# Two 64-row tiles for the values and scores of a cross-attention layer, and the sum of the values' halves in HBM

## What is computed

```python
q = x @ Wq + bq                       # 32 query heads of 32
k = ctx @ Wk + bk; v = ctx @ Wv + bv  # 8 key/value heads of 32, each shared by 4 query heads
p = softmax(q k^T / sqrt(32) + mask)  # over 64 keys
x = layernorm((p v) @ Wo + bo + x) * gamma + beta
```

## Time and profile before

| | |
|---|---|
| median of 3 runs | 1740.94 us |
| profiled execution, device time | 1740.28 us |
| its span in the profile | 1738.5 us |
| TensorE (PE) busy, share of the span | 98% |
| weight loads (PEld) | 82% |
| VectorE (DVE) | 67% |
| GpSimd (POOL) | 61% |
| ScalarE (ACT) | 33% |
| granted TensorE clock, mean | 0.998 |
| chain that ended last | PE 86%, DVE 6%, POOL 3%, DMA 2%, ACT 1%, issue 2% |

### The profile page before, as it was taken

One profiled execution on the slowest core, in us unless ns is written; L12 is line 12 of the kernel. 1 busy time (PEld: TensorE's weight loads), 2 busy tenths in 40 slices (PEclk: granted clock), 3 DMA queues, 4 the chain that ended last, 5 costly groups with the idle time before them and its releaser, 6 DMA issues.

```text
span 1738.5 us, 22384 instructions
## 1 busy us (share of the span) xinstructions
PE 1709.0 (98%) x8449; PEld 1428.8 (82%) x8449; DVE 1169.7 (67%) x1111; ACT 581.3 (33%) x669; POOL 1060.6 (61%) x587
## 2 busy tenths in 40 slices
PE   6999999999999899999999999999999999999998
PEld 6888888888888788888888877888888888888887
DVE  7999898898988656565656578446644664466443
ACT  4444354444444433333434223122312231223110
POOL 1777877877787766565766553446734673467331
PEclk9999999999999999999999999999999999999999
DMA  8443344332336577777776856556545654565432
GB/s 240 103 110 86 77 110 108 80 86 73 77 98 187 165 228 230 222 232 227 240 224 223 262 176 194 172 167 185 172 152 169 184 171 154 170 184 168 132 109 97
DMA packets 278127, 280.11 MB, mean 161 GB/s; under 512 B 62330, under 2 KB 230404, under 8 KB 278020
## 3 DMA queue, kind: packets, MB, share of 16 engines
q1 hardware_dynamic: 276672, 276.97, 52.6%
q10 hardware_dynamic: 1348, 1.71, 0.3%
HBM read 175.81 MB, written 102.76 MB: 160 GB/s over the span
## 4 chain that ended last, share of the span: by engine, by line
PE 86%; DVE 6%; POOL 3%; issue 2%; DMA 2%; ACT 1%; SPq 0%; POOLq 0%; DVEq 0%; ACTq 0%
PE ps L53 28%; PE ps L54 27%; PE ps L55 27%; PE ps L712 1%; PE ps L720 1%; POOL y L1428 1%; POOL xb L1414 1%; DMA ocr<-o_scratch 1%; POOL wqsl L1446 0%; DVE xT0r L1039 0%; DVE wq0l L1058 0%; DMA pd<-p_scratch 0%; DMA p_scratch<-prob 0%; DMA ctx<-in_ctx_dram 0%; PE ps L693 0%
## 5 line engine op out<-in xcount | busy, mean ns | idle before, releaser
L1465 POOL TENSOR_TENSOR x2Tl<-x2r,x2Th 128x1024 fp32r<-128x1024 f32 x31 | 74.5, 2404 | 275.1 <-ACT x2Th L972 275.1
L1244 DVE STREAM_TRANSPOSE x2r<-xd 128x1024 f32<-128x1024 f32 x32 | 68.8, 2150 | 200.6 <-PE ps L55 200.6
L1399 POOL TENSOR_TENSOR pr<-pr,small 128x1024 f32<-128x1024 f32 x64 | 121.9, 1904 | 97.3 <-DVE small L1132 97.2
L972 ACT CAST x2Th<-x2r 128x1024 fp32r<-128x1024 f32 x32 | 33.7, 1052 | 366.5 <-DVE x2r L1244 366.5
L1394 POOL TENSOR_TENSOR pr<-pr,small 128x1024 f32<-128x1024 f32 x64 | 121.9, 1905 | 11.3 <-DVE small L1110 9.2
L1414 POOL TENSOR_TENSOR xb<-xb,bo 128x1024 f32<-128x1024 f32 x32 | 76.9, 2402 | 71.7 <-DMA xb<-in_x_dram 71.6
L1428 POOL TENSOR_TENSOR y<-y,bet 128x1024 f32<-128x1024 f32 x31 | 74.4, 2400 | 56.9 <-DVE y L1162 56.9
L1106 DVE TENSOR_REDUCE small<-pr 128x16 f32<-128x1024 f32 x64 | 78.1, 1220 | 42.6 <-ACT pr L852 42.6
L53 PE MATMUL ps<-wo0h,oc0l 128*128 128x512 f32 x256 | 102.0, 398 | 0.0
L53 PE MATMUL ps<-wo0h,oc1l 128*128 128x512 f32 x256 | 101.6, 397 | 0.4 <-DVE y L1199 0.4
L53 PE MATMUL ps<-xT0h,wq0l 128*128 128x512 f32 x256 | 100.1, 391 | 1.1 <-DVE wq0l L1058 1.1
(11 more groups left out here) (381 smaller groups left out, 5441.9 us busy)
## 6 DMA issues: line engine op xcount, KB each, us to landing
xr<-in_x_dram SPq DMA_DIRECT2D x128, 128.0 KB, 2.9
o_scratch<-ot SPq DMA_DIRECT2D x256, 64.0 KB, 1.8
ocr<-o_scratch SPq DMA_DIRECT2D x16, 1024.0 KB, 7.7
xb<-in_x_dram SPq DMA_DIRECT2D x32, 512.0 KB, 6.6
a_scratch<-ost SPq DMA_DIRECT2D x64, 256.0 KB, 3.5
b_scratch<-ost SPq DMA_DIRECT2D x64, 256.0 KB, 6.2
xd<-x_scratch SPq DMA_DIRECT2D x128, 128.0 KB, 2.9
raw<-b_scratch SPq DMA_DIRECT2D x64, 256.0 KB, 5.8
```

The costliest lines, as they stand in the source:

```text
L1244: nc.vector.transpose(x2r[:].rearrange("p k (t j) -> p t k j", t=TPB), xd[:].rearrange("p t (i k) -> p t k i", k=KT)).then_inc(x2_turned, 1)
L1399: nc.gpsimd.tensor_tensor(heads(v), heads(v), mx.unsqueeze(2).to_broadcast([P, TPB * GRP, KEYS]), ALU.subtract)\
L1465: nc.gpsimd.tensor_tensor(x2T[1][:], x2r[:], f32(x2T[0][:]), ALU.subtract).then_inc(x2_lo, 1)
```

## The change

- Values: for each of two 64-row halves h of the contraction (two heads each) a 64x128 weight tile holds high and low parts of V side by side, so one pass yields high and low products in different output partitions: 4 pairs of matmuls, into two banks (`V[0]`, `V[1]`). `ot` doubles; its two 64-partition halves go to two scratches, "o" and "ol".
- Once per block GpSimd issues one DMA that adds "ol" to "o" in HBM; chunks wait for it (`o_sum`).
- Scores: each half of the rows serves two heads, 12 pairs of matmuls of 128 columns. The layout of S and the mask add's access pattern follow.
- Order on TensorE: six k-tiles, values, scores, two k-tiles. The values of units 62 and 63 come behind the output tiles of slots 66 and 67; ScalarE's `norm_columns` in slots 65 and 66.
- One `qs` buffer in place of two; its room is the second `ot`'s.
- Front: wk and wv are read with 8 rows of the contraction per partition in one piece, the context's transposes to match; its casts start after a quarter of the transposes and alternate with wk's; wk's low part moves to GpSimd; K and V are projected in halves of the contraction; an early ScalarE instruction brings the table load forward.

```diff
+def stored_in(u):
+    v = u - 4 if u < UNITS + 2 else u - 5
+    return [v] if 0 <= v < UNITS and u != UNITS + 2 else []
...
-        qs = [[at(f"qs{i}{x}", 152 + 4 * i + 2 * j, [P, TPB, P], F32R) for j, x in enumerate("hl")] for i in range(2)]
+        qs = [at(f"qs{x}", 152 + 2 * j, [P, TPB, P], F32R) for j, x in enumerate("hl")]
-        vb = [at(f"vb{i}", 164 + 2 * i, [P, 2, 2, P], F32R) for i in range(2)]
+        vb = [at(f"vb{i}", 164 + 2 * i, [P, 2, 2, 2, HD0], F32R) for i in range(2)]
-        ot = [at(f"ot{i}", 202 + 2 * i, [P, BLK]) for i in range(2)]
+        ot = [at(f"ot{i}", o, [P, 2, BLK]) for i, o in enumerate((202, 156))]
...
             def load_chunk(c):
-                for i in range(2):
-                    sp.wait_ge(o_st[i], 64 * 4 * (t + 1))
+                sp.wait_ge(o_sum, 16 * (t + 1))
...
-                if 4 <= u < UNITS + 4:
-                    v = u - 4
+                for v in stored_in(u):
                     sp.wait_ge(o_ev, v + 1)
-                    for a in range(4):
-                        sp.dma_start(d["o"][v // KT, v % KT].rearrange("(j p) c -> p j c", j=GRP)[:, :, P * a:P * (a + 1)],
-                                     ot[v % 2][32 * a:32 * (a + 1)].rearrange("p (j c) -> p j c", j=GRP)).then_inc(o_st[v % 2], 16)
+                    for i, name in enumerate(("o", "ol")):
+                        for a in range(2):
+                            rows = slice(64 * i + 32 * a, 64 * i + 32 * (a + 1))
+                            sp.dma_start(d[name][v // KT, v % KT].rearrange("(j p) (h a c) -> p h a j c", j=GRP, h=2, a=2)[:, :, a],
+                                         ot[v % 2][rows].rearrange("p h (j c) -> p h j c", j=GRP)).then_inc(o_st[v % 2], 16)
...
                 def values_of(v):
-                    after(pe, o_ev, v - 1)
-                    for c in range(2):
-                        last = three(nc, V[v % 2], ...)
+                    after(pe, o_ev, v)
+                    for n, (c, x) in enumerate(((0, 1), (0, 0), (1, 1), (1, 0))):
+                        for h in range(2):
+                            rows = slice(64 * h, 64 * (h + 1))
+                            last = nc.tensor.matmul(V[h], vb[v % 2][rows, c].rearrange("p x a d -> p (x a d)"),
+                                                    pT[v % 2][x][rows, c].rearrange("p j n -> p (j n)"), start=n == 0, stop=n == 3)
...
-                    query(range(0, 4))
-                if 4 <= u < UNITS + 4:
+                    query(range(0, 6))
+                if 4 <= u < UNITS + 2:
                     values_of(u - 4)
-                if u < UNITS:
-                    query(range(4, 6))
...
                     for m in range(TPB):
-                        last = three(nc, S[v % 2][:, 256 * m:256 * (m + 1)], ...)
+                        for n, (x, y) in enumerate(((1, 0), (0, 1), (0, 0))):
+                            for r in range(2):
+                                rows = slice(64 * r, 64 * (r + 1))
+                                last = nc.tensor.matmul(S[v % 2].rearrange("p (j m s) -> p j m s", j=GRP, m=TPB)[:, 2 * r:2 * r + 2, m], qs[x][rows, m],
+                                                        kb[v % 2][rows, 2 * r:2 * r + 2, y], start=n == 0, stop=n == 2)
...
                 if 1 <= u - UNITS < 3:
                     turn_norm(u - UNITS - 1)
+                if 2 <= u - UNITS < 4:
+                    values_of(u - 4)
...
-                    nc.scalar.copy(ot[v % 2][:].rearrange("p (j i m) -> p j i m", ...), V[v % 2]...)
+                    nc.scalar.copy(ot[v % 2][:].rearrange("p h (j i m) -> p (h j) i m", ...), VV...)
...
+                if u in (UNITS + 1, UNITS + 2):
+                    norm_columns(u - (UNITS + 1))
                 (the turned probabilities' cast)
-                if u in (UNITS + 2, UNITS + 3):
-                    norm_columns(u - (UNITS + 2))
...
             (GpSimd, head of slot u, ahead of L1390)
+                if u >= KT + 5 and u % KT == 5 and (u - 5) // KT <= NBLK:
+                    t = (u - 5) // KT - 1
+                    for i in range(2):
+                        pool.wait_ge(o_st[i], 64 * 4 * (t + 1))
+                    after(pool, o_sum, 16 * t)
+                    nc.gpsimd.dma_start(*(d[name][t].rearrange("g p c -> (g p c)").rearrange("(q e) -> q e", q=4 * P) for name in ("o", "ol")),
+                                        accum_op=ALU.add, max_dma_last_dim=4096).then_inc(o_sum, 16)
```

More of the change, by code:

```diff
@@ L592, in tensor @@
             nc.tensor.transpose(PJ[0][:, :KT + 2], brow[:], ident[:KT + 2, :KT + 2]).then_inc(b_turned, 1)
[L593 to L600, removed]
-            pe.wait_ge(b_done, 1)
[L602 to L608, removed]
+            for i in range(2):
+                pe.wait_ge(ctx_lo, 2 * i + 2)
+                pe.wait_ge(kv_lo, i + 1)
+                for h in range(2):
+                    for k in range(4 * i, 4 * i + 4):
+                        last = three(nc, V[h][:, :CTX], [wk[x][:, k, P * h:P * (h + 1)] for x in (0, 1)],
+                                     [ctxT[x][:, k] for x in (0, 1)], k == 0, k == KT - 1)
+                    if i:
+                        last.then_inc(k_done, 1)
+            pe.wait_ge(b_done, 1)
+            for i in range(2):
+                pe.wait_ge(kv_lo, i + 3)
+                for r in range(2):
+                    for k in range(4 * i, 4 * i + 4):
+                        last = three(nc, PJ[r], [ctxT[x][:, k, P * r:P * (r + 1)] for x in (0, 1)],
+                                     [wv[x][:, k] for x in (0, 1)], k == 0, k == KT - 1)
+                    if i:
+                        last.then_inc(v_done, 1)
             def slot(u):
@@ L819, in scalar @@
             act.dma_start(brow[KT:], w["bk0"].rearrange("(h p) -> h p", p=P)).then_inc(b_ld, 16)
+            act.wait_ge(ones, 3)
+            nc.scalar.copy(warm, mhalf)
             act.wait_ge(ctx_ld, 64)
[L821 to L825, removed]
+            act.dma_start(wvr[:], w["Wv0"].rearrange("(p k) n -> p k n", k=KT)).then_inc(kv_ld1, 16)
+            for n in range(2):
+                for i in (2 * n, 2 * n + 1):
+                    act.wait_ge(ctx_t, i + 1)
+                    nc.scalar.copy(ctxT[0][:, 2 * i:2 * i + 2, :], C2[:, HALF * i:HALF * (i + 1)]).then_inc(ctx_hi, 1)
+                if n == 0:
+                    act.dma_start(bv_row[:], row(w["bv0"], KV0)).then_inc(bv_ld, 16)
+                    act.wait_ge(kv_ld0, 16)
+                nc.scalar.copy(wk[0][:, half(n)], wkr[:, half(n)]).then_inc(kv_hi, 1)
             act.wait_ge(b_turned, 1)
             nc.scalar.copy(small[:, :KT + 2], PJ[0][:, :KT + 2]).then_inc(b_done, 1)
-            act.wait_ge(kv_ld0, 16)
-            for i in range(2):
-                nc.scalar.copy(wk[0][:, half(i)], wkr[:, half(i)]).then_inc(kv_hi, 1)
             act.wait_ge(kv_ld1, 16)
@@ L1140, in slot @@
                     dve.wait_ge(q_hi, u + 1)
[L1141 to L1142 removed]
+                    nc.vector.scalar_tensor_tensor(out=qs[1][:], in0=Q[u % 2].rearrange("p (n m) -> p m n", m=TPB), scalar=bq[:, u % KT:u % KT + 1],
+                                                   in1=f32(qs[0][:]), op0=ALU.add, op1=ALU.subtract).then_inc(q_lo, 1)
                 for g in wq_late(u):
@@ L1174, in split_wt @@
                 def split_wt(f, i):
+                    if f == 0 and i == 0:
+                        dve.wait_ge(o_st[1], 64 * UNITS // 2)
                     dve.wait_ge(wT_hi, 2 * f + i + 1)
@@ L1358, in gpsimd @@
             pool.wait_ge(ones, 5)
-            pool.wait_ge(kv_lo, 2)
+            for i in range(2):
+                pool.wait_ge(kv_hi, i + 1)
+                nc.gpsimd.tensor_tensor(wk[1][:, half(i)], wkr[:, half(i)], f32(wk[0][:, half(i)]), ALU.subtract).then_inc(kv_lo, 1)
             for i in range(2):
```

46 lines of the change are left out of this document (22 added, 24 removed).

## The result

The changed kernel takes 1785.05 us, median of 4 runs (1774.62 to 1786.84), beside 1741.2 us before on the same chip: ratio 1.0231, 95% interval 1.0213 to 1.0250. It is 2.3% slower; forecast were 1734.3 us and a range up to 1753. The profiled execution took 1785.89 us, its span is 1784.3 us.

What follows compares the result with a forecast made beforehand. It saw TensorE's stream and VectorE's loop running at the same pace, the loop setting the time up to unit 54. Terms: -2.1 - 2.0 - 5.5 + 3.0 = -6.6 us, giving 1734.3 us; range 1722 to 1753.

Steps and rivals of the forecast that it cites:

- Values, scores, round trip.: TensorE's unit: values 0.46 us less, scores 0.16 less, one round trip into 64-row tiles 0.41 more; 8.27 becomes 8.06 us.
- What that is worth ... 2.1 us.: Attention units: TensorE's shorter unit gains 0.4 us up to unit 54 and 1.7 in the last 8 units.
- Rival B: Attention units: TensorE's stream does set the time; 11 us more gain, 1723, or 1692 with scores at half price; chance 0.15.
- Stores. ... Zero.: Stores in the units: four DMAs as before with twice the bytes, SP's issue 0.47 us each; cost zero.
- The add in HBM.: Units 13 to 53: GpSimd's hold by the DMA issue, taken as 1.5 us, costs 6 x 0.5 = +3.0 us.
- rival A: Units: the add's issue holds GpSimd long; slower from 2.6 us of hold, 1749 us at 4; chance 0.25.
- Front ... all of it passed on.: Kernel's start: turns of x and first query come earlier; gain 1.3 to 2.4 us, 2.0 taken, all passed on.
- rival C: Seam: the stall only moves to tile 4 or the first projection, and the add costs 3 us; 1739; chance 0.10.
- Seam ... I take 5.5.: Between units and output tiles: the 4.2 us stall goes, tile 4 starts earlier; gain 2 to 6.2 us, 5.5 taken.
- two end terms: The front and the seam, at the two ends of the units: gains of 2.0 and 5.5 us.
- rival D: Units: the pairs of matmuls don't run side by side; 54 us slower, given as 1790; chance 0.02.

Runs made afterwards that it cites:

- before: The old kernel, without the change; 1741.2 us beside the changed kernel, 1741.7 to 1742.0 us beside the follow-up runs.
- e1: The changed kernel with the accumulating DMA left out; 1739.59 us, ratio 0.9984.
- e5: The changed kernel without the stores to ol_scratch, the per-block DMA adding a 2 MB block of x instead; 1746.57 us, ratio 1.0025.
- after: The changed kernel, with the whole change; 1785.05 us, ratio 1.0231.
- e2: The old kernel plus one accumulating DMA per block, adding a 2 MB block of x to o_scratch; 1754.43 us, ratio 1.0072.
- e6: The old kernel with the per-block add of x and its ot stores doubled, to two scratches; 1786.77 us, ratio 1.0261.
- e7: The old kernel with the change's front alone; 1743.85 us, ratio 1.0015.
- e10: The changed kernel with the ol_scratch stores issued by ScalarE instead of SP and no accumulating DMA; 1737.86 us, ratio 0.9976.
- e11: The changed kernel with the adds of blocks 1 to 7 moved into the stage of the output tiles; 1792.17 us, ratio 1.0284.
- e8: The old kernel with the change's seam alone; 1739.67 us, ratio 0.9989.
- e9: The changed kernel with the ol_scratch stores issued by ScalarE on its own queue instead of SP, add kept; 1751.01 us, ratio 1.0053.
- e4: The changed kernel with each block's DMA copying ol_scratch over o_scratch without adding; 1756.63 us, ratio 1.0072.
- e3: The changed kernel with the add in 64 DMAs of 256 KB, one per unit; 1749.64 us, ratio 1.0051.

## Why the prediction was wrong, step by step

- *Values, scores, round trip.* Right: 0.23 and 0.11 us a pair, unit 8.07 us for 8.06. Of the two rules weighed for the scores, the one on a load's columns (the Trainium skill, TensorE: Matmul & The Clock Gate, LDWEIGHTS) agrees with the pairs; twice the speed (the Trainium skill, TensorEngine Tiling (Array Packing), Theoretical Speedup) would be 0.06 a pair.
- *"What that is worth ... 2.1 us."* Right. From VectorE's max of unit 0 to its sum of unit 63, before takes 529.79 us, e1 527.79: 2.0 us, of which 0.5 between units 8 and 52 (0.4 was said) and 1.5 behind them (1.7). Rival B fell; the loop of VectorE sets the pace.
- *"Stores. ... Zero."* Wrong. It asked what waits for the landing, not what stands behind the stores in SP's list, and took 0.47 us an issue whatever the bytes; an issue of 128 KB takes 0.61 where one of 64 KB takes 0.43, so SP is issuing for 52.4 of 58 us instead of 46.8. Zero holds only without the add (e1). With the add, one store half more costs 38 us (e5 against after), 32 in the old kernel (e2 against e6).
- *"The add in HBM."* The failed step, with the one above. Its hold was bounded (0.47 to 5.33 us, 1.5 taken) and is 1.02 to 1.22, which is hidden, so that the term's +3.0 was 0; the lock by VectorE that rival A named from the Trainium skill (SBUF — State Buffer, the "DVE blocks DMA" trap) does not show in any of the 8 holds. But the transfer was never costed: 2 MB read, 2 MB read and added and written, 15.5 us at 74% of the engines, eight times, in a stage that before had a DMA share of 0.34. The row with the warning was in my hands: an SP issue held up for 5.33 us at full DMA in the front. I used it as a bound of GpSimd's hold, not as what a full set of engines does to SP. What the transfer did instead: at its bursts vb landed 9.0 to 14.9 us after SP began to issue it, where TensorE was ready after 4.3 to 11.8. Rival A had the right sign by the wrong mechanism.
- *Size of the loss.* Over the same units after takes 43.4 us more than e1. TensorE's waits for values and scores make 35.4 us (e1: 3.0), so 32 us are waiting. The other 11 are what is left of the matmuls at the 1.2 GHz level: TensorE is busy for 41.5 us in the five stretches where the granted clock is 0.50, and half of that, 21 us, is lost against full clock. An estimate: about 10 of these come back, since undisturbed units run at 8.07 to 8.10 us in after and at 8.3 on average in e1.
- *"Front ... all of it passed on."* Wrong. The first query came 1.2 us earlier (30.95 against 32.15), but VectorE's first max only came when it had before (44.77, before 44.76); with the same front it was 0.5 us later in e7, 1.2 in e1, 2.0 in e10 and 0.7 earlier in e11. Late next was kb, which goes through HBM: in e7 its stores were issued from 31.66 us (before: 32.43), its loads only from 39.15 (38.24). -2.0 was -0.7 to +2.0 at the first max, and +2.0 in e7's time.
- *"Seam ... I take 5.5."* The start of tile 4 right (5.45), what was passed on 2.1 (e8). In after, even that is eaten: VectorE's split of wT waits 4.67 us for the last store of ol_scratch, since ot shares wT's room (TensorE's 4.8 us above). The changed kernel has this wait in its text (L1191); the working passed it over.

Without the add the forecast would have been 1731.3 and e1 is 1739.6: the two end terms miss by 8 us. The other 45.5 are the add's. A slip that changed no chance: rival D's 54 us give 1795, not 1790.

What is shown is that the add and the doubled stores that SP issues multiply each other (e1, e2, e5, e6, e9). How the engines divide between two queues is read from the first burst only. That some bursts stall TensorE for 10 us and others for 1 is landing less lead, and mostly lead. Why the lead is short at some bursts and not at others, SP's time or the order of its list, is read from traces and tested by no run: one with SP's issues as many and as long but half the bytes, or the loads ahead of the stores in SP's list, would.

## What to carry to other kernels

Cost a DMA three times: its issue, its own landing, and what its bytes do to every transfer that shares the engines while it lasts; above all to small loads that are issued only a few us before their use. A mean DMA share of a third is no cover for a burst that is longer than the lead of the next load, so look at that lead burst by burst. When an edit earns time on TensorE and pays in DMA traffic, ask first whether TensorE sets the pace: here it earned 2 us and paid 45.

## What the runs showed of the hardware that was not expected

- An accumulating DMA from HBM to HBM of 2 MB takes 14.1 to 16.8 us to land (after, eight of them, median 15.5); a plain copy took 9.1 to 12.2 us (e4, median 10.4) and half the engine time.
- While it runs, SP's queue had 26% of the engines (after, 140 to 156 us), 16 KB loads of the units landed after up to 15.1 us where the median is 1.8 (kb), and single issues of SP took up to 5.65 us.
- SP's issue of a 128 KB store took 0.61 us, of a 64 KB store 0.43 (after and before, 80 to 138 us, medians).
- GpSimd's issue of such a DMA holds it 1.02 to 1.22 us for 2 MB, and 0.77 to 0.98 us for 256 KB (e3, median 0.79).
- Two of four stores moved to ScalarE's queue cost ScalarE two issues a unit and slowed nothing; without the add this order gave the lowest median of all runs (e10, 1737.86 us).
